# Openings of stages: GpSimd's memsets behind the first normalisations, PE's wait for them moved, integer weights loaded a stage earlier

## What is computed

```
x = x + attn_small(norm(x))    # 16 heads of 8, scores times a decay; k and v pass a latent of 32
x = x + experts(norm(x))       # a shared SwiGLU and 2 of 7 routed ones
x = x + attn_wide(norm(x))     # 32 heads of 32, then its own layer norm with gamma and beta
x = x + experts(norm(x))
x = x + attn_small2(norm(x))   # 16 heads of 8, with a position bias
x = x + swiglu_int(norm(x))    # weights are int32 in [-127, 127], times 1/127
x = x + linear_attn(norm(x))
x = x + swiglu_int(norm(x))    # the same integer weights
```

```
q, k, v = split(z @ Wqkv.T);  logits = q @ k.T * 8**-0.5 + bias;  out = softmax(logits) @ v @ Wout.T
gate = z @ (w_gate/127).T;  up = z @ (w_up/127).T;  out = (silu(gate) * up) @ (w_down/127).T
```

## Time and profile before

| | us |
|---|---|
| runs | 3969.84, 3965.29, 3964.39 (median 3965.29) |
| the profiled execution, its own time | 3969.8 |
| its span | 3968.0 |
| PE busy | 3408.2 (86%) |
| DVE busy | 3021.5 (76%) |
| ACT busy | 2470.1 (62%) |
| POOL busy | 1208.9 (30%) |
| mean granted PE clock | 0.937 of full speed |

### The profile page before, as it was taken

The page is one execution under the profiler, slowest core; times in us unless marked ns, Lnnn a source line. Parts: engine busy times, 40 slices in busy tenths (PEclk is TensorE's granted clock), DMA queues, the critical chain, the costliest instruction groups (busy, mean ns, idle before and its releaser), DMA issues. The chain is left out here.

```text
span 3968.0 us, 57665 instructions
## 1 busy us (share of the span) xinstructions
PE 3408.2 (86%) x18424; PEld 2106.2 (53%) x18424; DVE 3021.5 (76%) x7074; ACT 2470.1 (62%) x4540; POOL 1208.9 (30%) x922
## 2 busy tenths in 40 slices
PE   6888888687986999999999997879699999868875
PEld 3555555465753555555555554657466666543433
DVE  7999999666865776776776773668678888669985
ACT  4888888544742565565565563457379999752325
POOL 1000000034531665665665664545300000010111
PEclk9999999878996999999999998889899999988887
DMA  4222221112446666666666660133342222200000
GB/s 137 53 51 47 54 35 21 31 51 97 141 132 80 85 88 86 85 88 86 86 89 85 87 89 11 53 120 137 103 110 47 43 32 46 37 29 0 0 1 22
DMA packets 206308, 265.34 MB, mean 67 GB/s; under 512 B 95748, under 2 KB 107333, under 8 KB 205882
## 3 DMA queue, kind: packets, MB, share of 16 engines
q1 hardware_dynamic: 196282, 240.66, 34.4%
q0 software_dynamic: 9728, 20.99, 1.6%
HBM read 102.77 MB, written 57.08 MB: 40 GB/s over the span
## 5 line engine op out<-in xcount | busy, mean ns | idle before, releaser
L1252 DVE TENSOR_REDUCE at_b_top<-ps 128x1 f32<-128x512 f32 x1024 | 661.7, 681 | 343.9 <-PE ps L983 343.1
L1131 ACT ACTIVATE at_b_e<-ps 128x512 f32<-128x512 f32 x1024 | 582.1, 599 | 474.0 <-PE ps L995 461.7
L598 ACT ACTIVATE at_a_e<-at_a_logits,at_a_neg_top 128x512 f32<-128x512 f32 x1024 | 656.1, 716 | 120.1 <-DVE at_a_neg_top L658 118.5
L869 POOL TENSOR_TENSOR at_b_e_pair<-at_b_e 128x1024 f32<-128x1024 f32 x252 | 594.0, 2377 | 396.3 <-PE ps L1021 393.0
L518 PE MATMUL ps<-at_a_in_k,at_a_in_q 96*128 96x512 f32 x1024 | 476.5, 491 | 143.2 <-DVE at_a_clipped L626 118.5
L983 PE MATMUL ps<-at_b_k,at_b_q 96*128 96x512 f32 x1024 | 499.1, 493 | 33.2 <-DMA at_b_k<-at_b_k_hi 26.2
L995 PE MATMUL ps<-at_b_q,at_b_k 98*128 98x512 f32 x1024 | 423.7, 417 | 16.6 <-ACT at_b_e L1131 15.4
L654 DVE CUSTOM_DVE_ANT_0 at_a_logits<-ps,at_a_in_strip 128x512 f32<-128x512 f32 x512 | 340.6, 689 | 83.4 <-issue 33.4
L518 PEld LDWEIGHTS ps<-at_a_in_k,at_a_in_q 96*128 96x128 f32 x1024 | 184.4, 190 | 355.5 <-DVE at_a_clipped L626 209.2
L626 DVE TENSOR_SCALAR at_a_clipped<-ps 128x512 f32<-128x512 f32 x512 | 352.5, 689 | 19.7 <-PE ps L518 18.6
L466 POOL COPY at_a_v<-at_a_in_v_all 128x128 f32<-128x128 f32 x64 | 34.8, 548 | 1062.6 <-PE ps L541 1062.5
(11 more groups left out here) (348 smaller groups left out, 6493.3 us busy)
## 6 DMA issues: line engine op xcount, KB each, us to landing
moe_stage<-in_moe_w SPq DMA_DIRECT2D x46, 768.0 KB, 4.4
at_b_q<-at_b_q_hi SPq DMA_DIRECT2D x124, 256.0 KB, 5.7
at_b_k<-at_b_k_hi SPq DMA_DIRECT2D x124, 256.0 KB, 7.7
at_b_q<-at_b_q_lo SPq DMA_DIRECT2D x62, 256.0 KB, 7.6
at_b_k<-at_b_k_lo SPq DMA_DIRECT2D x62, 256.0 KB, 7.9
slot_rows<-empty_slots SPq DMA_DIRECT2D x44, 288.0 KB, 5.4
moe_xg<-slot_rows SPq DMA_DIRECT2D x44, 288.0 KB, 4.6
at_a_in_q<-q_hi SPq DMA_DIRECT2D x128, 64.0 KB
```

Source lines behind the costliest of these rows:

```text
L598: act.activation(e[:, j, qb, :], logits[:, j % 2, qb, :], ACT.Exp, bias=neg_top[:, j % 2, qb:qb + 1]).then_inc(exp_done, 1)
L869: pool.tensor_tensor(e_pair[:, j, :, :], e[r][:, j, 0:2, :], e[r][:, j, 2:4, :], ALU.add).then_inc(pair_done, 1)
L1131: act.activation(e[r][:, j, b, :], g.ps[:, shifted_bank(n, b), :], ACT.Exp).then_inc(exp_done, 1)
L1252: dve.tensor_reduce(top[:, t, j, qb:qb + 1], g.ps[:, bank, :], AX_X, ALU.max).then_inc(max_done, 1)
```

## The change

GpSimd waits in both small projections and in wide attention until DVE has issued and finished the four normalisations of batch 1 (`xn_done`), before its memsets. In wide attention PE's wait for the memsets (`set_up`) is taken from the start of its stream and put ahead of the first shifted score. The load of the integer weights, with its buffer and its semaphore, goes into an object of its own, and SP issues it at the start of `project_out` of the second small attention, ahead of the loads of `o`. That call is moved into the scope in which the weights' buffers live.

```diff
@@ project_small @@
             @block.gpsimd
             def _(pool):
+                pool.wait_ge(xn_done, TB)
                 ahead.zero(pool)
@@ attend_wide @@
             @block.gpsimd
             def _(pool):
 
+                pool.wait_ge(xn_done, TB)
                 for r in range(RQ):
                     pool.memset(k4[r][KROWS:KROWS + 2].bitcast(F32), -1.0).then_inc(set_up, 1)
                 pool.wait_ge(set_up, RQ + 1)
...
             @block.tensor
             def _(pe):
-                pe.wait_ge(set_up, RQ + 1)
                 pe.wait_ge(wide.loaded, 16 * wide.LOADS)
...
                 def shifted_scores(n, r, j, kb):
 
+                    if n == 1 and j == 0 and kb == 0:
+                        pe.wait_ge(set_up, RQ + 1)
                     if n > NG - 2:
@@ project_out @@
-def project_out(nc, g, name, w_out):
+def project_out(nc, g, name, w_out, ints=None):
...
                 @block.sync
                 def _(sp):
+                    if ints:
+                        ints.load(sp)
                     for n in range(1, B + 1):
@@ integer_swiglu @@
-def integer_swiglu(nc, g, name, packed, stats, w, ahead):
+class IntegerWeights:
+
+
+    def __init__(self, nc, stack, sems, packed):
+        self.packed = packed
+        self.stage = stack.enter_context(nc.sbuf_tensor("ffn_stage", [P, 3 * HID], I32))
+        self.loaded = sems.enter_context(nc.semaphore("ffn_stage_loaded"))
+
+    def load(self, sp):
+        sp.dma_start(self.stage[:], self.packed[0]).then_inc(self.loaded, 16)
+
+
+def integer_swiglu(nc, g, name, ints, stats, w, ahead):
...
-        stage = ph.sb("stage", [P, W], I32) if first else None
...
                 if first:
-                    sp.dma_start(stage[:], packed[0]).then_inc(w_loaded, 16)
                     ahead.load(sp)
...
                 if first:
-                    dve.wait_ge(w_loaded, 16)
-                    dve.tensor_scalar(stage_f[:], stage[:], 1.0, None, ALU.mult).then_inc(w_float, 1)
+                    dve.wait_ge(ints.loaded, 16)
+                    dve.tensor_scalar(stage_f[:], ints.stage[:], 1.0, None, ALU.mult).then_inc(w_float, 1)
@@ build @@
-                project_out(nc, g, "out_a1", a["a1_wo"])
-        with nc.sbuf_tensor("ffn_weights", [P, 3 * HID], F32R) as w:
+        with nc.sbuf_tensor("ffn_weights", [P, 3 * HID], F32R) as w, ExitStack() as whole:
+            ints = IntegerWeights(nc, whole, stack, a["ffn_w"])
+            project_out(nc, g, "out_a1", a["a1_wo"], ints)
...
-                quantised(5, w, ahead)
+                quantised(5, ints, w, ahead)
...
-            quantised(7, w, None)
+            quantised(7, None, w, None)
```

More of the change, by code:

```diff
@@ L1912, in integer_swiglu @@
         acc = ph.sb("acc", [P, S])
-        w_loaded, w_float, w_done, shift_done = (ph.sem(k) for k in ("w_loaded", "w_float", "w_done", "shift_done"))
+        w_float, w_done, shift_done = (ph.sem(k) for k in ("w_float", "w_done", "shift_done"))
         xn_done, xp_ready, x_hi_done, x_lo_done = (ph.sem(k) for k in ("xn_done", "xp_ready", "x_hi_done", "x_lo_done"))
@@ L2635, in row_stats_of, with quantised @@
             g.stats_ready = False
-        def quantised(k, w, ahead):
+        def quantised(k, ints, w, ahead):
             name = f"ffn{k}"
@@ L2640, in quantised @@
             with nc.sbuf_tensor(f"stats_{name}", [P, TILES, 6], F32) as stats:
-                integer_swiglu(nc, g, name, a["ffn_w"], stats, w, ahead)
+                integer_swiglu(nc, g, name, ints, stats, w, ahead)
                 if name != "ffn7":
```

## The result

The changed kernel took 3958.9 us, median of 20 runs (3953.86 to 3964.13). The kernel before, run beside it on the same chips, took 3969.61 us, median of 20 (3963.97 to 3973.17). The ratio is 0.9974 with an interval of 0.9967 to 0.998: faster by 10.7 us, 0.27%. The forecast was a gain of 10.2 us, 0.26%, and a time of 3955.1 us in a range of 3951.5 to 3961.5.

A forecast was written before the change was run, and what follows sets the result against it. No engine bounds the whole kernel; the edits shorten chains in stage openings. Terms 0.55 + 6.13 + 1.25 + 2.68 - 0.4 = 10.2 us off the median 3965.29 give 3955.1 us, range 3951.5 to 3961.5.

The forecast's parts named there:

- term 1: First small projection's opening: normalisations ahead of memsets let the weight fold start earlier, until loads are late; gain 0.55 us.
- term 5: Second small attention's output projection: integer-weight load issued ahead costs 0.4 us, bounds 0.3 and 3.9 us.
- Term 2: Wide attention's opening: fast normalisations and PE's moved memset wait start transposes earlier; gain 6.13 us, between 3.2 and 6.3.
- The prediction's own marks: Signs of being right in wide attention: transposes about 1.2 us into the stage, first score some 21.6 us after its start.
- rival 2: Wide attention: memsets hold the first low parts, costing 2.9 us; 7.3 us gained, 3958.0 us; chance 8%.
- Rival 3: Wide attention's opening absorbs half its gain because its transfers end no earlier; 7.1 us gained, 3958.2 us; chance 7%.
- Term 3: Second small projection's opening: earlier transposes, then the flip matrix is late next; gain 1.25 us, bounds 0.6 and 1.5.
- rival 4: Wide attention's body: shifted work brings TensorE's 1.2 GHz clock into it, making the kernel slower, 3981.1 us; chance 5%.
- Term 4: Integer stage's opening: conversion no longer waits for its weight load, copy of x starts earlier; gain 2.68 us, bounds 2.0 and 3.0.
- The last projection longer by over 1 us: A sign that the prediction is wrong, in the second small attention's output projection, where the moved load is issued.
- rival 1: Output projection with the moved load: first transfers are late and stay late, 3.5 us; 6.7 us gained, 3958.6 us; chance 10%.
- Rival 5: Stage openings: last normalisations of the first batch still run beside the first memset; 1.2 us off, 3956.3 us; no chance given.

The follow-up runs named there:

- e7: The kernel before, unchanged, traced a second time in a single execution: 3968.23 us, beside 3968.76 for one of the kernel before.
- e9: The changed kernel itself again, on the chip of e8: 3959.82 us, median of 11, ratio 0.9974 to the kernel before.
- e1: Changed kernel with PE's wait for the wide-attention memsets back at the start of its stream: 3965.06 us, single execution; wide attention 1260.60 us.
- e5: Changed kernel with PE repeating four transposes while waiting for the flip matrix in the second small projection: 3950.66 us, single execution; that stage 41.24 us.
- e2: Changed kernel without GpSimd's wait before the wide-attention memsets, PE's moved wait kept: 3969.6 us, single execution; wide attention 1257.09 us.
- e10: e8 plus added PE transposes of the identity as filling in both small projections: 3951.99 us, median of 5, ratio 0.9957 to the kernel before.
- e3: Changed kernel with the integer-weight load issued behind the other 33 loads of the output projection: 3967.74 us, single execution; that projection 26.20 us.
- e4: Changed kernel with the second small projection's flip matrix loaded first, on its own semaphore: 3966.03 us, single execution; that stage 40.11 us.
- e8: Changed kernel with edits of e3 and e4, plus first small projection's loads in order of use: 3955.5 us, median of 5, ratio 0.9966 to kernel before.

## Why the prediction was right, and where it was off

**The absolute number.** The sum of 10.2 us met 10.7. That it came so near is in part luck: term 1 gave 0.7 us more than forecast and term 5 took 0.4 to 0.6 more, which nearly cancel, and the other three were right to 0.2. The time was off by 3.8 us because the prediction held the profiled execution for the slow one of three and took the terms off the median of 3965.29. Over 20 runs the kernel before takes 3969.61; the profiled execution (3969.8) was the typical one, and its own 3959.6 would have been 0.7 us from the result. For the same reason 3958.9 is not under the 3957.4 that the prediction drew for "faster", though 0.27% is more than its 0.2%.

**Term 1 (0.55).** The mechanism held: the load is late next, PE waits 1.73 us for it, and the second batch starts 0.58 us earlier than in the first trace. The stage gave 1.3 to 1.4 in the mean, which the prediction could not have from one trace. Four normalisations end with the second memset or with the third (e7), and the change ends that: they take 1.1 us in all ten traces that have it. Against e7 the first store comes 1.8 us earlier in the profiled execution and 2.5 in e9. Against the first trace it gained only 0.3 in the profiled execution, which goes with the clock's rise at 14.3 us for 13.1; in e1, with the rise at 11.2, it gained 1.2.

**Term 2 (6.13).** Right in each link: 1.11 us, PE 1.7 us into the stage, the first score 6.04 us earlier, and the memsets were done long before the moved wait. (The prediction's own marks, 1.2 and 21.6 us, count from the first normalisation, at 1195.83; from there the trace has 1.26 and 21.64.) The two bounds of the low parts are settled: 0.69 us each beside a memset, so the earlier trace rows was the right row and rival 2 is false. The rule of the Trainium skill (SBUF — State Buffer, Who interferes with whom) is that a DVE instruction with one SBUF input, outside the 2-port modes, doesn't contend with GpSimd. It agrees with this trace. Rival 3 is false too: the dense transfers moved with the low part that triggers them, and the stage kept all 6 us.

**Term 3 (1.25).** The flip matrix was late next, and the second batch came 1.33 us earlier. The stage kept 0.8 in the pairs and 1.2 by all six traces, between 0.8 and 2.2 in single ones. In the profiled pair the first projections run at the lower clock in both kernels, and its rise, 12.9 us into the stage for 13.0, did not move with them; the shorter ones of the six are those with an earlier rise. That the clock's rise is a term of an opening is what the prediction left out; its rival 4 looked for the clock in the body of wide attention, where nothing changed. e5 gives its size, in one execution: 1.5 to 2.9 us, more than the term.

**Term 4 (2.68).** 2.69 us at the copy of x. The conversion took 0.99 us for 0.76 beside the two short memsets, inside the 0.4 allowed, and ScalarE's queue covered it. The stage gained 3.2 in the pairs. Most of the other 0.5 is the load: in e7 it landed 4.6 us after its issue, not 3.9, so that the copy of x started 6.86 us into the stage for 6.15 in the first trace, and 3.46 in all ten with the change. The link is worth 3.0 in the mean of the pairs. The two executions with the late rise of the clock (e2, e10) bring the mean of all ten down to 2.9.

**Term 5 (-0.4) was mis-sized: it measured about -1.0** (-0.8 by the pairs, 1.05 us came back in e3, and five traces without the load ahead stand 1.0 under seven with it). "The last projection longer by over 1 us" was one of the prediction's own signs of being wrong, and the profiled pair shows it: 27.25 for 26.21. The step that failed is "cost 0.4 us" for the issue, with what is late on the DMA engines made up. SP's own next issues became slower, by 0.58 and 0.13 us, and they belong to the stream that paces the stage, so nothing makes them up. The small pieces also came later: the first transposes start 5.83 us into the stage (3451.36), before 4.57. The rule of the Trainium skill (DMA: Bandwidth & Descriptors, Queues, rings and completion order) is that a DMA engine takes a ring's descriptors in order. It points the right way: the first piece landed 3.5 to 3.8 us after its issue in the seven traces with the load ahead, and 2.3 in the five without. The full 1.9 us of the prediction's estimate did not come, and rival 1, of 3.5 us, is false.

**Rival 5** (the last normalisations beside the first memset) is false: the four take 1.11 us and GpSimd starts at their end in all three stages.

Open: what makes the clock rise at 4.8 us in e4's in_a1 and at 9.1 us in e8 with the same code; whether in e5 the closed gap or the added work brought it forward; why the filling did not do so in in_a0; and why ffn5 has the late rise in two executions of ten.

## What to carry to other kernels

Read a stage's opening as a chain and ask of each shortened link what is late next; the terms then add up, here to 0.27% of the whole, with two errors that cancelled. Two things belong in that chain beside the waits: what an added DMA does to the issues behind it on the same queue (put a load that has a whole stage of time behind the urgent ones, not ahead), and when the clock of TensorE rises, for a stage that ends a nearly fixed time behind its first store keeps most of what is gained ahead of that store. Where PE idles a us between two short bursts in an opening, try to close that gap or fill it, and look at the granted clock of the windows behind it, in more than one execution.

And trace the unchanged kernel more than once: the second trace of it moved the first projection by 1.9 us and showed four normalisations held by three memsets, where the first trace had two.

## What was not expected of the hardware

- An idle time of 0.97 us of PE in an opening went with a granted clock of 0.51 for the next 7 us; filled with transposes that nothing reads, the same window had 1.00, and the stage was 2.8 us shorter than the pair after and 1.5 shorter than the shortest of the six (e5, one execution).
- Four normalisations beside the memsets took 3.8 us in one execution and 5.6 in another of the same program, ending with the second and with the third memset.
- A 576 KB load ahead of four 64 KB ones and the weight's made the issues of these five take 3.5 to 4.0 us on SP in seven traces, for 2.6 to 3.1 in the five without it.
- The expert stages, with the same code, took between 395.5 and 406.1 us, a spread as large as what the whole change is worth.
- ffn5 took 65.96 to 66.28 us in eight executions and 68.20 and 68.36 in two, with the clock's rise 8.1 to 8.9 us into it in the eight and at 10.4 and 10.7 in the two.
